# Attention output by three passes of rounded hi and lo operands in place of one fp32 product, in a gated cross-attention and FFN kernel on one core

## The chip, the core and the metric

The kernel runs on one core of a Trainium2 chip. The metric is the device time of one execution in microseconds (us), as the median of several runs. A core has five engines with a queue each, which work strictly in their own order and meet at semaphores: TensorE (PE in the profile, PEld for its weight loads), VectorE (DVE), ScalarE (ACT), GpSimd (POOL) and SyncE (SP), which here issues the large DMAs.

## The reference

For each of 16 batches of 128 rows and 256 columns, with one attention head (the code is cut to what matters):

```python
xn = layernorm(x)
Q = xn @ Wq.T + bq
K = ctx @ Wk.T + bk
scores = where(mask, -inf, Q @ K.T)
attn = softmax(scores)
x1 = x + tanh(g_xattn) * ((attn @ ctx) @ Wo.T + bo)
w = (weights >= 0) * 2.0 - 1.0
y = clip((layernorm(x1) @ w.T) * scale + bias, -100, 100)
out = x1 + tanh(g_ffn) * y
```

All inputs and outputs are fp32.

## The kernel before

The batches go through in 8 groups of two (G = 8, GB = 2). Wq and Wk are folded into one matrix at the start, so that scores = xn times K_sb, where K_sb comes from the context. The context is multiplied with Wo first (Z = ctx x Wo^T, scaled by the gate), and so the attention output is O = P^T x Z, divided by the row sums of P in the residual step on VectorE.

TensorE runs a loop of rounds, written out by hand. In round i it does, in this order: `scores(i)`, the transposes of the context (i+1), of x1 (i-1) and of the normalised x (i+1), `project_Z(i)`, `project_K(i+1)`, `transpose_p(i)`, `ffn(i-1)` and `attend(i)`. The mask's small product at the head of `scores` carries the wait for the group before.

Several products are already made with operands in two parts: ScalarE copies a PSUM result to a tile of type float32r (the rounded hi part), VectorE subtracts that from the PSUM bank and writes the rest (the lo part). `split_cT` and `split_x1T` do so for the context and for x1. `project_Z` and `project_K` then take three products hi x hi, hi x lo and lo x hi, each one pass of TensorE. `attend` is one of the two places in a round that still use full fp32 operands (the other is `scores`): ScalarE copies Z (`evict_Z`) and the transposed P (`evict_PT`) as they are, and two matmuls of fp32 follow, one for each batch. In the trace each such fp32 matmul has two records.

ScalarE's order in round i: cT_hi (i+1), the two exponentials (i), x1T_hi (i-1), xT (i+1), Z (i), PT (i), K (i+1). VectorE's order: `residual(i-1)` (reciprocal, then x1 from ps_O), `max_of_scores(i)`, `scale_ffn_out(i-2)`, `split_cT(i+1)`, `stats_x1(i-1)`, `split_x1T(i-1)`, then the statistics of groups of x that the table `STATS_AT` puts there (groups 2 and 3 in round 0, 4 and 5 in round 1, 6 in round 2, 7 in round 3, none later), and `final(i-2)`, which adds x1 to the clipped FFN output. GpSimd does the small layer norm steps, the normalised x (`xn`), `add_bo`, `bias_and_clip`.

The tile x1_sb has the name x_sb in some rows of the profile, and the lower half of the bank ps_S holds the scores and its upper half the transposed P (`ps_PT`), so that the transposes of P are rows of ps_S.

Of the kernel before, what the change touches and what calls it, by code (L numbers as in the profile page):

```python
# [13 lines left out]
P = 128  # L14
# [7 lines left out]
def gated_xattn_ffn(nc, x, ctx, mask, g_xattn, g_ffn, wq, bq, wk, bk, wo, bo, w_ffn, scale_ffn, bias_ffn, out):  # L22
# [9 lines left out]
    GB = 2  # L32
# [15 lines left out]
    with ExitStack() as stack:  # L48
# [3 lines left out]
        def sem(name):  # L52
            return stack.enter_context(nc.semaphore(name))

        def bank(name):
# [30 lines left out]
        xT = sb("xT", [P, 2, DC, T])  # L86
        cT_hi, cT_lo = sb("cT_hi", [P, 2, DC, T], F32R), sb("cT_lo", [P, 2, DC, T], F32R)
        K_sb = sb("K_sb", [P, 2, DC, T])
        Z_sb = sb("Z_sb", [P, 2, GB, D])
        p_sb, PT_sb = sb("p_sb", [P, 2, GB, P]), sb("PT_sb", [P, 2, GB, P])  # L90
        x1T_hi, x1T_lo = sb("x1T_hi", [P, 2, DC, T], F32R), sb("x1T_lo", [P, 2, DC, T], F32R)


# [43 lines left out]
        bn_x_done, mv_x_done, ve_x_done, rstd_x_done, mr_x_done, off_x_done, xn_done = (  # L137
            sem(n) for n in ("bn_x_done", "mv_x_done", "ve_x_done", "rstd_x_done", "mr_x_done", "off_x_done", "xn_done"))
        bn_1_done, mv_1_done, ve_1_done, rstd_1_done = (sem(n) for n in ("bn_1_done", "mv_1_done", "ve_1_done", "rstd_1_done"))
        cT_hi_done, cT_lo_done, xT_done, K_done, Z_done, PT_done = (  # L140
            sem(n) for n in ("cT_hi_done", "cT_lo_done", "xT_done", "K_done", "Z_done", "PT_done"))
        nmax_done, p_done, recip_done, xb_done, x1_done, x1T_hi_done, x1T_lo_done = (
            sem(n) for n in ("nmax_done", "p_done", "recip_done", "xb_done", "x1_done", "x1T_hi_done", "x1T_lo_done"))
        f_scaled_done, f_biased_done, f_clip_done, out_done = (
# [29 lines left out]
        @block.scalar  # L174
        def _(act):
            act.dma_start(bq_col[:], bq.rearrange("(p c) -> p c", c=DC)).then_inc(bqk_loaded, 16)
            act.dma_start(bk_col[:], bk.rearrange("(p c) -> p c", c=DC)).then_inc(bqk_loaded, 16)
            for k, v in enumerate((g_xattn, g_ffn)):
                act.dma_start(gate_row[:, k:k + 1], row(v)).then_inc(gate_loaded, 16)
            act.dma_start(mask_u8[:], mask).then_inc(mask_loaded, 16)  # L180
            for tile, v in ((bo_row, bo), (sc_row, scale_ffn), (bi_row, bias_ffn)):
                act.dma_start(tile[:], row(v)).then_inc(rows_loaded, 16)

            def evict_cT_hi(g):
                act.wait_ge(cT_prod, g + 1)
                nc.scalar.copy(cT_hi[:, g % 2], ps_cT).then_inc(cT_hi_done, 1)  # L186

            def evict_xT(g):
                act.wait_ge(xT_prod, g + 1)
                nc.scalar.copy(xT[:, g % 2], ps_xT).then_inc(xT_done, 1)  # L190

            def evict_K(g):
                act.wait_ge(kbias_ready, 1)
                act.wait_ge(K_prod, g + 1)
                for c in range(DC):
                    nc.scalar.activation(K_sb[:, g % 2, c], ps_K[:, c], ACT.Identity, bias=kbias[:, c:c + 1]  # L196
                                         ).then_inc(K_done, 1)

            def evict_Z(g):
                act.wait_ge(Z_prod, g + 1)  # L200
                nc.scalar.copy(Z_sb[:, g % 2], ps_Z).then_inc(Z_done, 1)

            def exp(g):
                act.wait_ge(nmax_done, g + 1)
                for b in range(GB):
                    r = g * GB + b
                    nc.scalar.activation(p_sb[:, g % 2, b], ps_S[b], ACT.Exp, bias=nmax[:, r:r + 1],  # L207
                                         accum_out=psum_p[:, r:r + 1]).then_inc(p_done, 1)

            def evict_PT(g):  # L210
                act.wait_ge(PT_prod, g + 1)
                nc.scalar.copy(PT_sb[:, g % 2], ps_PT).then_inc(PT_done, 1)

            def evict_x1T_hi(g):
                act.wait_ge(x1T_prod, g + 1)
                nc.scalar.copy(x1T_hi[:, g % 2], ps_x1T).then_inc(x1T_hi_done, 1)

            evict_cT_hi(0)
            for c in range(DC):
                act.wait_ge(ps_wqk_ready, c + 1)  # L220
                nc.scalar.copy(wqk_hi[:, c], ps_wqk[c]).then_inc(wqk_hi_ready, 1)
            act.wait_ge(ps_kbias_ready, 1)
            nc.scalar.copy(kbias[:], s_bank[:, 0:DC]).then_inc(kbias_ready, 1)
            act.wait_ge(ps_gate_ready, 1)
            nc.scalar.activation(tanh_g[:], o_bank[:, 0:2], ACT.Tanh).then_inc(tanh_ready, 1)
            act.wait_ge(tanh_ready, 1)
            act.wait_ge(ps_woT_ready, 1)
            nc.scalar.activation(woT_hi[:], ps_woT, ACT.Identity, scale=tanh_g[:, 0:1]).then_inc(woT_hi_ready, 1)
            evict_K(0)
            evict_xT(0)  # L230
            act.wait_ge(ps_rows_ready, 1)
            nc.scalar.activation(bo_g[:], x1T_bank[:, 0:D], ACT.Identity, scale=tanh_g[:, 0:1]).then_inc(bo_g_ready, 1)
            for i in range(G + 1):
                if i + 1 < G:
                    evict_cT_hi(i + 1)
                if i < G:
                    exp(i)
                if i >= 1:
                    evict_x1T_hi(i - 1)
                if i + 1 < G:  # L240
                    evict_xT(i + 1)
                if i < G:
                    evict_Z(i)
                    evict_PT(i)
                if i + 1 < G:
                    evict_K(i + 1)
                if i == 0:
                    nc.scalar.activation(sc_g[:], x1T_bank[:, D:2 * D], ACT.Identity, scale=tanh_g[:, 1:2]
                                         ).then_inc(sc_g_ready, 1)
                    act.wait_ge(ps_bi_ready, 1)  # L250
                    nc.scalar.activation(bi_g[:], f_bank[:, 0:D], ACT.Identity, scale=tanh_g[:, 1:2]).then_inc(bi_g_ready, 1)
                    act.wait_ge(ps_wT_ready, 1)
                    nc.scalar.copy(wT[:], ps_x1T).then_inc(wT_ready, 1)
# [86 lines left out]
        def _(dve):  # L340
# [20 lines left out]
            def split_cT(g):  # L361
                dve.wait_ge(cT_hi_done, g + 1)
                nc.vector.tensor_tensor(cT_lo[:, g % 2], ps_cT, cT_hi[:, g % 2].bitcast(F32), ALU.subtract
                                        ).then_inc(cT_lo_done, 1)

            def split_x1T(g):
                dve.wait_ge(x1T_hi_done, g + 1)
                nc.vector.tensor_tensor(x1T_lo[:, g % 2], ps_x1T, x1T_hi[:, g % 2].bitcast(F32), ALU.subtract  # L368
                                        ).then_inc(x1T_lo_done, 1)
# [55 lines left out]
            for i in range(G + 2):  # L425
                if 1 <= i <= G:
                    residual(i - 1)
                if i < G:
                    max_of_scores(i)
                if i >= 2:  # L430
                    scale_ffn_out(i - 2)
                if i == 0:
                    dve.wait_ge(w_loaded, 16)
                    nc.vector.tensor_scalar(w_sign2[:], w_sb[:], 0.0, 2.0, ALU.is_ge, ALU.mult).then_inc(sign2_done, 1)
                    dve.wait_ge(sign2_done, 1)
                    nc.vector.tensor_reduce(w_sum[:], w_sign2[:], AX.X, ALU.add).then_inc(w_sum_done, 1)
                if i + 1 < G:
                    split_cT(i + 1)
                if i == 0:
                    dve.wait_ge(w_sum_done, 1)  # L440
                    nc.vector.tensor_scalar(w_mean[:], w_sum[:], 1.0 / D, None, ALU.mult).then_inc(w_mean_done, 1)
                    dve.wait_ge(w_mean_done, 1)
                    for c in range(DC):
                        nc.vector.tensor_scalar(w_cent[:, c], w_sign2[:, c], w_mean[:, c:c + 1], None, ALU.subtract
                                                ).then_inc(w_cent_ready, 1)
                if 1 <= i <= G:
                    stats_x1(i - 1)
                    split_x1T(i - 1)
                for g in STATS_AT.get(i, ()):
                    stats_x(g)  # L450
                if i >= 2:
                    final(i - 2)

        @block.tensor
        def _(pe):
# [45 lines left out]

            def project_Z(g):
                if g >= 1:
                    pe.wait_ge(Z_done, g)
                else:
                    pe.wait_ge(woT_lo_ready, 1)
                for b in range(GB):
# [6 lines left out]

            def scores(g):
                if g >= 1:
                    pe.wait_ge(PT_done, g)
                else:
                    pe.wait_ge(kbias_ready, 1)
                    pe.wait_ge(mask_ready, 1)  # L520
# [14 lines left out]
                last.then_inc(PT_prod, 1)  # L535

            def attend(g):
                pe.wait_ge(PT_done, g + 1)
                pe.wait_ge(Z_done, g + 1)
                if g >= 1:  # L540
                    pe.wait_ge(x1_done, GB * g)
                else:
                    pe.wait_ge(tanh_ready, 1)
                for b in range(GB):
                    last = nc.tensor.matmul(ps_O[:, b], PT_sb[:, g % 2, b], Z_sb[:, g % 2, b], start=True, stop=True)  # L545
                last.then_inc(O_prod, 1)

            def ffn(g):
# [88 lines left out]
```

## Time and profile before

| | |
|---|---|
| median of 3 runs | 87.29 us (87.25 to 87.45) |
| the profiled execution | 87.51 us |
| its span, first to last instruction | 85.8 us |
| TensorE busy | 71.8 us (84%), 528 matmul records |
| VectorE busy | 52.8 us (62%) |
| ScalarE busy | 36.8 us (43%) |
| GpSimd busy | 58.8 us (69%) |
| one round in the middle of the loop | 7.46 us |

Busy shares are averages over a start of about 14 us, eight rounds and an end of about 11 us. What sets the time is the chain of waits, which names for each stretch the engine whose work ended last. The profiled execution took 87.51 us, 0.22 us more than the median of the runs; 1.71 us of it lie outside the span.

### The profile page before, as it was taken

What the parts mean: (1) busy time and instruction counts of PE and PEld (TensorE: products, weight loads), DVE (VectorE), ACT (ScalarE), POOL (GpSimd) and SP (SyncE); (2) the same over time, 40 slices, a digit from 0 to 9 for tenths busy, and PEclk for the clock granted to TensorE, in tenths of its full rate; (3) what the DMA queues carried; (4) which work ended last, traced back from release to release, by engine and by line L of the source; (5) the groups of instructions that cost most, each with busy time, mean ns of one, the idle gap of its engine ahead of it and who ended that gap; (6) DMA issues with size and microseconds to landing.
All of it is one profiled execution on the core that took longest, in us unless ns stands there. A gap on an engine that the chain in (4) does not pass through costs nothing.

```text
span 85.8 us, 1574 instructions
## 1 busy us (share of the span) xinstructions
PE 71.8 (84%) x528; PEld 65.5 (76%) x528; DVE 52.8 (62%) x153; ACT 36.8 (43%) x98; POOL 58.8 (69%) x105
## 2 busy tenths in 40 slices
PE   2999999597799999999999999999999996635000
PEld 2999997495599979979997997999799795414000
DVE  0057764895059849938974980894498187594430
ACT  0142547655629507552950855395085436020000
POOL 5002888934892905889999688999998819568740
PEclk9999999999999999999999999999999999999555
DMA  0899999920000000030003003000300300300303
GB/s 24 253 344 370 349 348 349 348 72 0 0 0 0 0 0 11 0 113 17 0 0 122 8 0 122 0 0 0 122 8 0 122 0 0 110 12 0 122 0 122
DMA packets 7697, 7.44 MB, mean 87 GB/s; under 512 B 775, under 2 KB 7434, under 8 KB 7690
## 3 DMA queue, kind: packets, MB, share of 16 engines
q1 hardware_dynamic: 7360, 7.34, 26.3%
q8 instruction: 4, 0.07, 0.3%
q10 hardware_dynamic: 330, 0.01, 0.2%
q14 instruction: 3, 0.02, 0.1%
HBM read 5.25 MB, written 2.10 MB: 86 GB/s over the span
## 4 chain that ended last, share of the span: by engine, by line
PE 63%; POOL 14%; DVE 8%; issue 5%; DMA 5%; POOLq 1%; ACTq 0%; DVEq 0%
PE ps_K L465 12%; PE ps_Z L465 11%; PE ps_S L526 9%; PE ps_O L545 8%; PE ps_F L465 8%; DMA bk_col<-in_L_xattn_bk_dram 5%; PE ps_xT L460 4%; PE ps_x1T L460 4%; PE ps_cT L460 3%; POOL xn L284 3%; POOL f_biased L302 3%; POOL mask_sel L318 2%; DVE f_scaled L391 2%; PE ps_S L534 2%; PE ps_S L521 2%
## 5 line engine op out<-in xcount | busy, mean ns | idle before, releaser
L302 POOL TENSOR_TENSOR f_biased<-f_scaled,bi_g 128x256 f32<-128x256 f32 x16 | 11.4, 734 | 8.6 <-DVE f_scaled L391 8.6
L383 DVE SCALAR_TENSOR_TENSOR x_sb<-ps_O,recip_p,xb_sb 128x256 f32<-128x256 f32 x16 | 7.0, 479 | 14.1 <-PE ps_O L545 11.9
L186 ACT CAST cT_hi<-ps_cT 128x512 fp32r<-128x512 f32 x8 | 4.7, 585 | 17.9 <-PE ps_cT L460 17.9
L296 POOL TENSOR_TENSOR xb_sb<-x_sb,bo_g 128x256 f32<-128x256 f32 x16 | 11.3, 727 | 0.0
L465 PE MATMUL ps_F<-wT,x1T_hi 128*128 128x256 f32 x32 | 8.7, 304 | 2.3 <-DVE x1T_lo L368 2.3
L284 POOL TENSOR_SCALAR xn<-x_sb,rstd_x,off_x 128x256 f32<-128x256 f32 x16 | 9.9, 624 | 0.5
L465 PE MATMUL ps_Z<-woT_hi,cT_hi 128*128 128x256 f32 x32 | 9.6, 299 | 0.0
L526 PE MATMUL ps_S<-K_sb,xT 128*128 128x128 f32 x64 | 9.3, 288 | 0.0
L465 PE MATMUL ps_K<-cT_hi,wqk_hi 128*128 128x256 f32 x32 | 9.1, 284 | 0.0
L465 PE MATMUL ps_K<-cT_hi,wqk_lo 128*128 128x256 f32 x32 | 9.0, 282 | 0.0
L465 PE MATMUL ps_K<-cT_lo,wqk_hi 128*128 128x256 f32 x32 | 9.0, 281 | 0.0
L465 PE MATMUL ps_Z<-woT_lo,cT_hi 128*128 128x256 f32 x32 | 8.9, 277 | 0.0
L465 PE MATMUL ps_Z<-woT_hi,cT_lo 128*128 128x256 f32 x32 | 8.9, 277 | 0.0
L526 PEld LDWEIGHTS ps_S<-K_sb,xT 128*128 128x128 f32 x64 | 7.7, 191 | 1.1 <-ACT xT L190 0.2
L545 PE MATMUL ps_O<-Z_sb,PT_sb 128*128 128x256 f32 x32 | 8.2, 378 | 0.0
L465 PEld LDWEIGHTS ps_F<-wT,x1T_hi 128*128 128x128 f32 x32 | 6.0, 188 | 2.8 <-DVE x1T_lo L368 2.8
L465 PE MATMUL ps_F<-wT,x1T_lo 128*128 128x256 f32 x32 | 8.0, 282 | 0.0
L396 DVE TENSOR_TENSOR out_sb<-f_clip,x_sb 128x512 f32<-128x512 f32 x8 | 5.5, 691 | 3.8 <-POOL f_clip L306 3.8
L391 DVE SCALAR_TENSOR_TENSOR f_scaled<-ps_F,rstd,sc_g 128x256 f32<-128x256 f32 x16 | 6.9, 475 | 0.9 <-POOL rstd L291 0.9
L269 POOL TENSOR_SCALAR ve_x<-mv_x 128x4 f32<-128x4 f32 (+1 forms) x5 | 1.5, 292 | 8.8 <-DVE mv_x L349 8.6
L196 ACT ACTIVATE K_sb<-ps_K,kbias 128x256 f32<-128x256 f32 x16 | 6.7, 477 | 0.7 <-PE ps_K L465 0.7
L207 ACT ACTIVATE p_sb<-ps_S,nmax 128x128 f32<-128x128 f32 x16 | 5.8, 369 | 2.5 <-DVE nmax L373 2.5
(94 smaller groups left out, 193.5 us busy)
## 6 DMA issues: line engine op xcount, KB each, us to landing
ctx_sb<-in_ctx_dram SPq DMA_DIRECT2D x8, 256.0 KB, 6.5
x_sb<-in_x_dram SPq DMA_DIRECT2D x8, 256.0 KB, 6.3
out_dram<-out_sb SPq DMA_DIRECT2D x8, 256.0 KB, 2.1
wq_sb<-in_L_xattn_Wq_dram SPq DMA_DIRECT2D x1, 256.0 KB, 3.0
wk_sb<-in_L_xattn_Wk_dram SPq DMA_DIRECT2D x1, 256.0 KB, 3.8
wo_sb<-in_L_xattn_Wo_dram SPq DMA_DIRECT2D x1, 256.0 KB, 4.8
w_sb<-in_L_ffn_weights_dram SPq DMA_DIRECT2D x1, 256.0 KB, 5.6
bq_col<-in_L_xattn_bq_dram ACTq DMA_DIRECT2D x1, 1.0 KB, 3.2
```

Source lines behind the costliest of these rows:

```text
L196: nc.scalar.activation(K_sb[:, g % 2, c], ps_K[:, c], ACT.Identity, bias=kbias[:, c:c + 1]).then_inc(K_done, 1)
L207: nc.scalar.activation(p_sb[:, g % 2, b], ps_S[b], ACT.Exp, bias=nmax[:, r:r + 1], accum_out=psum_p[:, r:r + 1]).then_inc(p_done, 1)
L284: nc.gpsimd.tensor_scalar(xn[:, g % 3, b], x_sb[:, r], rstd_x[:, r:r + 1], off_x[:, r:r + 1], ALU.mult, ALU.add).then_inc(xn_done, 1)
L296: nc.gpsimd.tensor_tensor(xb_sb[:, r], x_sb[:, r], bo_g[:], ALU.add).then_inc(xb_done, 1)
L302: nc.gpsimd.tensor_tensor(f_biased[:, r], f_scaled[:, r], bi_g[:], ALU.add).then_inc(f_biased_done, 1)
L383: nc.vector.scalar_tensor_tensor(out=x1_sb[:, r], in0=ps_O[:, b], scalar=recip_p[:, r:r + 1], in1=xb_sb[:, r], op0=ALU.mult, op1=ALU.add). ...
L391: nc.vector.scalar_tensor_tensor(out=f_scaled[:, r], in0=ps_F[:, b], scalar=rstd_1[:, r:r + 1], in1=sc_g[:], op0=ALU.mult, op1=ALU.mult).t ...
L396: nc.vector.tensor_tensor(out_sb[:, rows(g)], f_clip[:, g % 2], x1_sb[:, rows(g)], ALU.add).then_inc(out_done, 1)
L460: last = nc.tensor.transpose(dst[:, c, b * P:(b + 1) * P], src[:, b, c * P:(c + 1) * P], ident[:])
L465: last = nc.tensor.matmul(dst, lhsT, rhs, start=(n == 0), stop=(n == len(pairs) - 1))
L526: last = nc.tensor.matmul(ps_S[b], xT[:, g % 2, c, b * P:(b + 1) * P], K_sb[:, g % 2, c, b * P:(b + 1) * P], start=False, stop=(b == GB - ...
L545: last = nc.tensor.matmul(ps_O[:, b], PT_sb[:, g % 2, b], Z_sb[:, g % 2, b], start=True, stop=True)
```

## The change

Z and the transposed P are now kept in two rounded parts each. ScalarE's two copies write float32r tiles Z_hi and PT_hi. VectorE gets two new instructions in every round, `split_Z(i)` behind `split_x1T(i-1)` and ahead of the statistics, and `split_PT(i)` behind the statistics and ahead of `final(i-2)`. `attend` makes three products for each batch in place of one, and waits for the lo parts.

```diff
-        Z_sb = sb("Z_sb", [P, 2, GB, D])
-        p_sb, PT_sb = sb("p_sb", [P, 2, GB, P]), sb("PT_sb", [P, 2, GB, P])
+        Z_hi, Z_lo = sb("Z_hi", [P, 2, GB, D], F32R), sb("Z_lo", [P, 2, GB, D], F32R)
+        p_sb = sb("p_sb", [P, 2, GB, P])
+        PT_hi, PT_lo = sb("PT_hi", [P, 2, GB, P], F32R), sb("PT_lo", [P, 2, GB, P], F32R)
...
-                nc.scalar.copy(Z_sb[:, g % 2], ps_Z).then_inc(Z_done, 1)
+                nc.scalar.copy(Z_hi[:, g % 2], ps_Z).then_inc(Z_hi_done, 1)
...
-                nc.scalar.copy(PT_sb[:, g % 2], ps_PT).then_inc(PT_done, 1)
+                nc.scalar.copy(PT_hi[:, g % 2], ps_PT).then_inc(PT_hi_done, 1)
...
+            def split_Z(g):
+                dve.wait_ge(Z_hi_done, g + 1)
+                nc.vector.tensor_tensor(Z_lo[:, g % 2], ps_Z, Z_hi[:, g % 2].bitcast(F32), ALU.subtract
+                                        ).then_inc(Z_lo_done, 1)
+
+            def split_PT(g):
+                dve.wait_ge(PT_hi_done, g + 1)
+                nc.vector.tensor_tensor(PT_lo[:, g % 2], ps_PT, PT_hi[:, g % 2].bitcast(F32), ALU.subtract
+                                        ).then_inc(PT_lo_done, 1)
...
                 if 1 <= i <= G:
                     stats_x1(i - 1)
                     split_x1T(i - 1)
+                if i < G:
+                    split_Z(i)
                 for g in STATS_AT.get(i, ()):
                     stats_x(g)
+                if i < G:
+                    split_PT(i)
                 if i >= 2:
                     final(i - 2)
...
-                    pe.wait_ge(Z_done, g)
+                    pe.wait_ge(Z_lo_done, g)
...
-                    pe.wait_ge(PT_done, g)
+                    pe.wait_ge(PT_lo_done, g)
...
-                pe.wait_ge(PT_done, g + 1)
-                pe.wait_ge(Z_done, g + 1)
+                pe.wait_ge(PT_lo_done, g + 1)
+                pe.wait_ge(Z_lo_done, g + 1)
...
-                    last = nc.tensor.matmul(ps_O[:, b], PT_sb[:, g % 2, b], Z_sb[:, g % 2, b], start=True, stop=True)
+                    p_hi, p_lo, z_hi, z_lo = (t[:, g % 2, b] for t in (PT_hi, PT_lo, Z_hi, Z_lo))
+                    last = accumulate(ps_O[:, b], [(p_hi, z_hi), (p_hi, z_lo), (p_lo, z_hi)])
```

On VectorE, the rows of round 1 from the lo part of x1 on stood like this before (`bn_x` and `mv_x` are the statistics of groups 4 and 5, the last row is the x1 of group 1):

```order
L368 TENSOR_TENSOR x1T_lo<-ps_x1T,x1T_hi 128x512
L345 BN_STATS bn_x<-x_sb 128x6 x2
L349 BN_AGGR mv_x<-bn_x 128x2 x2
L345 BN_STATS bn_x<-x_sb 128x6 x2
L349 BN_AGGR mv_x<-bn_x 128x2 x2
L377 RECIPROCAL recip_p<-psum_p 128x2
L383 SCALAR_TENSOR_TENSOR x_sb<-ps_O,recip_p,xb_sb 128x256 x2
```

And so they stand in the changed kernel:

```order
L380 TENSOR_TENSOR x1T_lo<-ps_x1T,x1T_hi 128x512
L370 TENSOR_TENSOR Z_lo<-ps_Z,Z_hi 128x512
L347 BN_STATS bn_x<-x_sb 128x6 x2
L351 BN_AGGR mv_x<-bn_x 128x2 x2
L347 BN_STATS bn_x<-x_sb 128x6 x2
L351 BN_AGGR mv_x<-bn_x 128x2 x2
L375 TENSOR_TENSOR PT_lo<-ps_S,PT_hi 128x256
L389 RECIPROCAL recip_p<-psum_p 128x2
L395 SCALAR_TENSOR_TENSOR x_sb<-ps_O,recip_p,xb_sb 128x256 x2
```

The subtraction for P, on which `attend` of the same round waits, stands behind both groups of statistics.

On TensorE, the end of round 1 in the changed kernel, from the last product of the FFN on, reads so (before, one row `L545 MATMUL ps_O<-Z_sb,PT_sb 128x256 x2` stood in place of the six products into ps_O):

```order
L481 MATMUL ps_F<-wT,x1T_lo 128x256
L481 MATMUL ps_O<-Z_hi,PT_hi 128x256
L481 MATMUL ps_O<-Z_lo,PT_hi 128x256
L481 MATMUL ps_O<-Z_hi,PT_lo 128x256
L481 MATMUL ps_O<-Z_hi,PT_hi 128x256
L481 MATMUL ps_O<-Z_lo,PT_hi 128x256
L481 MATMUL ps_O<-Z_hi,PT_lo 128x256
```

Nothing else moves on TensorE; ScalarE and GpSimd keep their order.

## Rows read from the trace of the kernel before

**Rows 1.** The page, part 4: the chain that ended last, by engine.

```profile
PE 63%; POOL 14%; DVE 8%; issue 5%; DMA 5%; POOLq 1%; ACTq 0%; DVEq 0%
```

**Rows 2.** The chain in order of time, round 6: start us, us, what.

```profile
63.33 1.38 PE ps_Z L465 x12
...
67.32 0.87 PE ps_O L545 x4
```

**Rows 3.** Timeline of TensorE: attend of rounds 0, 1, 2, 6, 7; once what follows.

```profile
22.40 1.03 PE L545 MATMUL ps_O<-Z_sb,PT_sb 128*128 128x256 f32 x4
...
29.86 1.03 PE L545 MATMUL ps_O<-Z_sb,PT_sb 128*128 128x256 f32 x4
...
37.32 1.03 PE L545 MATMUL ps_O<-Z_sb,PT_sb 128*128 128x256 f32 x4
...
67.16 1.03 PE L545 MATMUL ps_O<-Z_sb,PT_sb 128*128 128x256 f32 x4
68.12 0.28 PE L521 MATMUL ps_S<-mask_sel,ones_b 16*128 16x258 bf16 x1
...
73.30 1.03 PE L545 MATMUL ps_O<-Z_sb,PT_sb 128*128 128x256 f32 x4
```

**Rows 4.** Timeline of VectorE and TensorE, round 7: a product that waited for a lo part.

```profile
71.52 0.66 DVE L368 TENSOR_TENSOR x1T_lo<-ps_x1T,x1T_hi 128x512 fp32r<-128x512 f32 x1
...
72.24 0.39 PE L465 MATMUL ps_F<-wT,x1T_hi 128*128 128x256 f32 x1 [0.72 <-DVE x1T_lo L368]
72.46 0.28 PE L465 MATMUL ps_F<-wT,x1T_lo 128*128 128x256 f32 x1
```

**Rows 5.** Timeline of ScalarE and VectorE, round 1: a split that waited for its hi part.

```profile
25.20 0.58 ACT L186 CAST cT_hi<-ps_cT 128x512 fp32r<-128x512 f32 x1 [2.02 <-PE ps_cT L460]
...
25.81 0.69 DVE L363 TENSOR_TENSOR cT_lo<-ps_cT,cT_hi 128x512 fp32r<-128x512 f32 x1 [0.62 <-ACT cT_hi L186]
26.42 0.74 DVE L355 BATCH_NORM_STATS2 bn<-x_sb 128x6 f32<-128x256 f32 x2
```

**Rows 6.** Groups of instructions (busy us, mean ns of one): a split of 256 columns.

```profile
L413 DVE TENSOR_TENSOR wqk_lo<-ps_K,wqk_hi 128x256 fp32r<-128x256 f32 x1 | 0.4, 425 | 0.0
```

**Rows 7.** Timeline of ScalarE: copies of Z (L201) and PT (L212), rounds 0, 1, 2 and 6.

```profile
18.70 0.58 ACT L201 COPY Z_sb<-ps_Z 128x512 f32<-128x512 f32 x1 [0.80 <-PE ps_Z L465]
...
27.45 0.59 ACT L201 COPY Z_sb<-ps_Z 128x512 f32<-128x512 f32 x1
...
34.91 0.58 ACT L201 COPY Z_sb<-ps_Z 128x512 f32<-128x512 f32 x1
36.56 0.37 ACT L212 COPY PT_sb<-ps_S 128x256 f32<-128x256 f32 x1 [1.07 <-PE ps_S L534]
...
66.40 0.37 ACT L212 COPY PT_sb<-ps_S 128x256 f32<-128x256 f32 x1 [1.07 <-PE ps_S L534]
```

**Rows 8.** Timeline of VectorE behind split_x1T, in rounds 1 and 2.

```profile
27.87 0.74 DVE L345 BATCH_NORM_STATS2 bn_x<-x_sb 128x6 f32<-128x256 f32 x2
...
29.60 0.13 DVE L377 RECIPROCAL recip_p<-psum_p 128x2 f32<-128x2 f32 x1
...
35.40 0.74 DVE L345 BATCH_NORM_STATS2 bn_x<-x_sb 128x6 f32<-128x256 f32 x2
```

**Rows 9.** Timeline of GpSimd and VectorE: rounds 2 and 3, then round 5.

```profile
37.57 1.09 POOL L284 TENSOR_SCALAR xn<-x_sb,rstd_x,off_x 128x256 f32<-128x256 f32 x2
...
39.03 0.69 POOL L291 TENSOR_TENSOR rstd<-ve,half 128x2 f32<-128x2 f32 x1
...
40.02 0.86 DVE L391 SCALAR_TENSOR_TENSOR f_scaled<-ps_F,rstd,sc_g 128x256 f32<-128x256 f32 x2
...
58.70 1.62 POOL L284 TENSOR_SCALAR xn<-x_sb,rstd_x,off_x 128x256 f32<-128x256 f32 x2
58.74 0.69 DVE L396 TENSOR_TENSOR out_sb<-f_clip,x_sb 128x512 f32<-128x512 f32 x1 [0.73 <-POOL f_clip L306]
```

More of the change, by code:

```diff
@@ L139, in gated_xattn_ffn @@
         bn_1_done, mv_1_done, ve_1_done, rstd_1_done = (sem(n) for n in ("bn_1_done", "mv_1_done", "ve_1_done", "rstd_1_done"))
-        cT_hi_done, cT_lo_done, xT_done, K_done, Z_done, PT_done = (
-            sem(n) for n in ("cT_hi_done", "cT_lo_done", "xT_done", "K_done", "Z_done", "PT_done"))
+        cT_hi_done, cT_lo_done, xT_done, K_done, Z_hi_done, Z_lo_done, PT_hi_done, PT_lo_done = (
+            sem(n) for n in ("cT_hi_done", "cT_lo_done", "xT_done", "K_done", "Z_hi_done", "Z_lo_done", "PT_hi_done",
+                             "PT_lo_done"))
         nmax_done, p_done, recip_done, xb_done, x1_done, x1T_hi_done, x1T_lo_done = (
```

## The prediction

> **What bounds the kernel now.** I read the page's chain first: 63% of it is TensorE, GpSimd and VectorE have 14% and 8% [rows 1]. In the order of time those two stand at the start and the end, and from round 1 to round 6 the chain is TensorE alone, piece by piece, with `attend` as one piece of 0.87 us for its two fp32 products [rows 2]. The timeline of TensorE says the same: `attend` begins at 29.86 in round 1 and at 37.32 in round 2, 7.46 us apart, and by round 6 at 67.16, five times 7.46 after round 1 [rows 3]. So whatever TensorE is spared in a round comes off the time, and whatever it is made to wait is added, as long as nothing else is as late. Then I looked for what `attend` will wait for: the two copies on ScalarE [rows 7] and VectorE's place in its own order [rows 8].
>
> **What is removed.** Two fp32 products cost 0.87 us [rows 2]. In their place come six products of 256 columns of float32r. The same shape and type, with the same pattern of operands, is `project_Z`: 12 in 1.38 us, 0.115 us each [rows 2], so six cost 0.69 us, and 0.18 us a round are spared. The other end is 0.12 us for one: from 72.46 to 73.30 lie seven slots [rows 3, 4], which would spare 0.15. I take 0.18 for the same operand pattern; in eight rounds that is 1.44 us. ScalarE's two copies stay as long as they were: a rounding copy of 512 columns took 0.58 us, the plain one 0.58 to 0.59 [rows 5, 7].
>
> **What is added.** Two subtractions a round on VectorE, and with them a longer way to `attend`. Its prices:
> - From the end of a copy on ScalarE to a waiting split: copy 25.20 + 0.58 = 25.78, split at 25.81, so 0.03 us [rows 5].
> - `split_Z`, 512 columns: the next instruction starts 0.61 us after the split (25.81 to 26.42) [rows 5].
> - `split_PT`, 256 columns: 0.42 us to its end, by the same subtraction out of a PSUM bank at that width [rows 6]. It can't be above the 0.69 of twice the width [rows 5].
> - From the end of a split to a waiting TensorE: 71.52 + 0.66 = 72.18, and the records start at 72.24, 0.06 later. The second product starts 0.22 after the first where a slot is 0.12, so 0.10 us of the first weight load lie open [rows 4]. Together 0.16.
> - The statistics of two groups: 27.87 to 29.60, 1.73 us [rows 8], so 0.87 for one group.
>
> Round 1, the dear one. Z_hi is there at 27.45 + 0.59 + 0.03 = 28.07 [rows 7], while VectorE is free at 27.87 [rows 8]. `split_Z` from 28.07 to 28.68, two groups of statistics to 30.41, `split_PT` to 30.83, first product of `attend` in effect at 30.99. It stood at 29.86 [rows 3]: 1.13 us of stall, less 0.18, **+0.95**.
>
> Rounds 2 and 3, one group each. Z_hi at 34.91 + 0.58 + 0.03 = 35.52, against 35.40 where VectorE is free; `split_Z` to 36.13, statistics to 37.00. PT_hi would allow 36.56 + 0.37 + 0.03 = 36.96 [rows 7], so the statistics are 0.04 late; `split_PT` to 37.42, product at 37.58, before 37.32. Stall 0.26, less 0.18: +0.08, twice, **+0.16**.
>
> Rounds 4 to 6, no statistics. `split_Z` is over before P is transposed. PT_hi at 66.40 + 0.37 + 0.03 = 66.80 [rows 7], `split_PT` to 67.22, product at 67.38, before 67.16 [rows 3]. Stall 0.22, less 0.18: +0.04, three times, **+0.12**. The FFN products between the transposes of P and `attend` hide the copy today with some room, but not the copy and a subtraction.
>
> Round 0 has two groups of statistics too, but TensorE waits there anyway for the constants of the FFN. `split_Z` from 18.70 + 0.58 + 0.03 = 19.31, with both statistics to 21.65, `split_PT` to 22.07, released at 22.13; `attend` starts at 22.40 [rows 3, 7]. No stall, **-0.18**. If that cover were gone, nothing before 22.40 would change, since 0.27 us are left.
>
> Round 7: the split of x1 ends at 72.18, `split_Z` and `split_PT` behind it take some 0.61 + 0.42, less the overlap of 0.06 with the end of the one before, to 73.15, product at 73.31 against 73.30 today, because the FFN products have waited for VectorE themselves [rows 3, 4]. No stall, **-0.18**.
>
> Sum: 0.95 + 0.16 + 0.12 - 0.18 - 0.18 = +0.87 us. On the profiled execution of 87.51 that is 88.38; it stood 0.22 above the median of the runs, so **88.2 us** against 87.29.
>
> **What is moved.** `final(i-2)` and the reciprocal now stand behind `split_PT`, ahead of the x1 of the round, which waits for ps_O. In round 2 they end at 37.42 + 0.69 + 0.13 = 38.24 [rows 8, 9], and `attend` is not over before 37.58 + 0.69 = 38.27. Hidden, with next to nothing left in full lengths; real starts overlap a little, which helps. If it is not hidden, it costs what it overhangs, 0.1 us a round. The waits of `project_Z` and `scores` for the lo parts of the round before are met long before.
>
> A second effect of the move: `final` reads two tiles of SBUF. In round 5 it lay over `xn` on GpSimd, and the pair took 1.62 us where the same pair takes 1.09 in round 2 [rows 9]. Now it starts about 37.36 in round 2, over the `xn` at 37.57, so rstd of group 1 ends at 39.03 + 0.69 + 0.53 = 40.25, when VectorE wants it at 40.02 + 0.08 = 40.10 [rows 9]. 0.15 late; round 3's `split_Z` has 0.12 of room (35.52 less 35.40, one round on), so 0.03 are left. I count it at nothing, 0.15 at most. The Trainium skill (SBUF — State Buffer, "SBUF: two separate sides") has a rule for it: a VectorE instruction with two SBUF inputs and a GpSimd one that reads SBUF lock each other out of a shared port for a whole instruction. By that rule the added splits, with one input in PSUM, hold nobody. The 0.53 us of round 5 agree with the rule, less than a whole `final` because the two started nearly together.
>
> **Rivals.**
> (a) Faster: the weight loads of the rounded products are pulled forward. Today the mask's product follows `attend` after 0.96 us (67.16 to 68.12), 0.09 more than the 0.87 of the piece [rows 2, 3]. If float32r products let the mask's load go early, 0.09 come off seven times, 0.63; if the first load of `attend` isn't open after a wait, 0.10 off six times, 0.60. Together -1.23, which gives +0.87 - 1.23 = -0.36, 86.9 us. It decides the sign from 0.87 on. Against it stands the waiting product whose load was open [rows 4]. The Trainium skill (TensorE: Matmul & The Clock Gate, the table of specs at its head) says that TensorE's queue pulls weight loads ahead of running matmuls within a window. Applied to the mask's load alone, that would make the sum +0.24. Chance of the whole 0.08, of one half (87.5 to 87.6) 0.10.
> (b) Slower by more: VectorE becomes the chain. If a subtraction out of the bank of P took up to 0.69, the six stalls grow by 0.27 each, and the shifted `final` and reciprocal overhang by as much: +1.6, 89.8 us. For it: VectorE has hardly 0.03 us left at 38.24. Against: the price at this width is in the trace [rows 6]. A tenth of a microsecond more a round, 88.8, is likelier than the whole. Chance of more than 88.9: 0.09.
> (c) No net change: VectorE takes the statistics of round 1 early enough. That would need 0.95 us of the stall to vanish; it leaves -0.08, 87.2 us. For it speaks only that the statistics are not needed so soon; their place in the order is fixed, in front of `split_PT`. Chance 0.05.
> The forecast itself, 87.8 to 88.9, has 0.68.
>
> **How the numbers follow.** The bounds of the unknown prices: 0.15 for 0.18 adds 0.24; the late rstd adds up to 0.15; an overhang of 0.1 in six rounds adds 0.6, hence 88.9 above with some of them together. Below, the half of (a) that concerns the first load gives 87.56, the other half 87.53; the range ends at 87.4 and leaves out the whole of (a) and (c). It holds 0.68 + 0.10 and a little. A measurement of this kernel tells about 0.2% from no change, 0.17 us: faster is below 87.12, slower above 87.46. Faster: the whole of (a) and part of (c), 0.11. Same: the rest of (c) and the lower edge of the halves, 0.07. Slower: 0.82.
>
> **What the changed kernel's profile would show.** TensorE in round 1: a gap of about 1.1 us between the last FFN product and the first product into ps_O, released by PT_lo; its releaser right ahead of it on VectorE the statistics. Gaps of about 0.2 in rounds 2 to 6, none in rounds 0 and 7. Rounds of 7.5 us where they were 7.46, round 1 about 8.4. Six products into ps_O in 0.69 us. `split_PT` rows of 0.42, `split_Z` of 0.66 to 0.69. I am wrong if round 1 has no such gap, if the mask's product follows the last product of `attend` sooner than it did, or if the x1 of a round starts later after `attend` than now, which would show `final` in the way.

## The result, and the profile after

| | before | changed |
|---|---|---|
| profiled execution | 87.51 us | 88.65 us |
| median of the runs | 87.27 us (4) | 88.96 us (4, 88.29 to 91.11) |
| changed over before | | 1.0147, 95% interval 1.0095 to 1.0199 |
| both again, beside experiments 5, 6 and 9 | 87.33 us (18) | 88.52 us (6), 1.0143, interval 1.0116 to 1.0170 |

The kernel became 1.4% slower. Executions over 1.5% longer than the fastest of their kernel, most of them with a lower granted clock of TensorE, stand in the medians but in no ratio; without its 91.11 the changed kernel has a median of 88.65 us. The profiled executions stand 1.14 us apart, the spans 1.1 us (86.9 and 85.8), and the ratios make it 1.25 to 1.28 us. The prediction had +0.87 us and 88.2.

The chain that ended last, part 4 of the page of the changed kernel:

```profile
PE 57%; POOL 14%; DVE 11%; issue 5%; DMA 4%; ACT 3%; POOLq 1%; ACTq 0%; DVEq 0%
```

TensorE held 63% before [rows 1]. VectorE has gained three points, and ScalarE comes in. Where that happened is to be seen in the rounds. The stretches below run from one mask product to the next, rounds 1 to 6 (columns: us of the stretch, then busy us and instructions of PE, PEld, DVE, ACT and POOL, granted clock, share and rate of the DMAs):

```profile
23.13:31.55 8.42, 7.58 (x62) 7.12 (x61) 6.25 (x20) 3.96 (x11) 6.25 (x12) 1.00 0.00 1
31.55:39.14 7.59, 7.59 (x62) 7.15 (x62) 6.68 (x19) 3.96 (x11) 4.64 (x8) 1.00 0.02 3
39.14:46.73 7.59, 7.59 (x63) 7.15 (x62) 6.69 (x19) 3.95 (x11) 7.15 (x13) 1.00 0.10 36
46.73:54.27 7.54, 7.54 (x63) 7.11 (x62) 5.92 (x15) 3.95 (x11) 6.28 (x11) 1.00 0.11 37
54.27:61.84 7.57, 7.57 (x63) 7.14 (x62) 5.93 (x15) 3.97 (x11) 7.13 (x13) 1.00 0.10 35
61.84:69.39 7.55, 7.55 (x62) 7.12 (x62) 6.21 (x15) 3.96 (x11) 6.10 (x10) 1.00 0.11 37
sum 46.26, PE 45.42 PEld 42.78 DVE 37.68 ACT 23.74 POOL 37.56; mean PE 7.57 PEld 7.13 DVE 6.28 ACT 3.96 POOL 6.26
```

A round took 7.46 us before, six of them 44.76; now they take 46.26, +1.50. Of this +0.96 are in round 1, +0.13 each in rounds 2 and 3, +0.08 to +0.11 in the others. Note that "PE busy" fills rounds 2 to 6 completely although there is a stall in each of them: the ends of products are modelled in the profile and cover a gap of this size. Only the distance of starts shows it.

TensorE's timeline at the end of round 1, and of round 6 (68.23 is the last product of the FFN):

```profile
29.52 0.28 PE L481 MATMUL ps_F<-wT,x1T_lo 128*128 128x256 f32 x1
30.64 0.39 PE L481 MATMUL ps_O<-Z_hi,PT_hi 128*128 128x256 f32 x1 [0.84 <-DVE PT_lo L375]
30.87 0.28 PE L481 MATMUL ps_O<-Z_lo,PT_hi 128*128 128x256 f32 x1
...
31.34 0.28 PE L481 MATMUL ps_O<-Z_hi,PT_lo 128*128 128x256 f32 x1
31.55 0.28 PE L537 MATMUL ps_S<-mask_sel,ones_b 16*128 16x258 bf16 x1
...
68.23 0.28 PE L481 MATMUL ps_F<-wT,x1T_lo 128*128 128x256 f32 x1
68.48 0.38 PE L481 MATMUL ps_O<-Z_hi,PT_hi 128*128 128x256 f32 x1
68.70 0.28 PE L481 MATMUL ps_O<-Z_lo,PT_hi 128*128 128x256 f32 x1
...
69.39 0.28 PE L537 MATMUL ps_S<-mask_sel,ones_b 16*128 16x258 bf16 x1
```

Here a slot is the distance of two starts in the stream. In round 1 the first product of `attend` starts 1.12 us after the last one of the FFN, where a slot is 0.12; its weight load lies open for another 0.11 (30.64 to 30.87 in place of 0.12). In round 6 it is 0.25 and 0.10. From the second product to the sixth it goes by 0.12 (30.87 to 31.34), and the mask's product follows the last one after 0.21, so 0.09 us of its load lie open as before [rows 2, 3]. The rows of the weight loads (PEld) in round 1 show it directly:

```profile
31.23 0.19 PEld L481 LDWEIGHTS ps_O<-Z_hi,PT_lo 128*128 128x128 f32 x1
31.55 0.09 PEld L537 LDWEIGHTS ps_S<-mask_sel,ones_b 16*128 16x128 bf16 x1
```

The load of the last product of `attend` starts 0.11 us ahead of its product (31.34), the mask's load together with its product (31.55).

VectorE's timeline in round 1, and in round 6, from `split_Z` on:

```profile
27.86 0.69 DVE L370 TENSOR_TENSOR Z_lo<-ps_Z,Z_hi 128x512 fp32r<-128x512 f32 x1
28.46 0.74 DVE L347 BATCH_NORM_STATS2 bn_x<-x_sb 128x6 f32<-128x256 f32 x2
...
30.20 0.39 DVE L375 TENSOR_TENSOR PT_lo<-ps_S,PT_hi 128x256 fp32r<-128x256 f32 x1
30.50 0.16 DVE L389 RECIPROCAL recip_p<-psum_p 128x2 f32<-128x2 f32 x1
...
68.00 0.42 DVE L375 TENSOR_TENSOR PT_lo<-ps_S,PT_hi 128x256 fp32r<-128x256 f32 x1 [0.75 <-ACT PT_hi L214]
68.34 1.12 DVE L408 TENSOR_TENSOR out_sb<-f_clip,x_sb 128x512 f32<-128x512 f32 x1
69.39 0.15 DVE L389 RECIPROCAL recip_p<-psum_p 128x2 f32<-128x2 f32 x1
69.60 0.88 DVE L395 SCALAR_TENSOR_TENSOR x_sb<-ps_O,recip_p,xb_sb 128x256 f32<-128x256 f32 x2
```

In round 1 nothing is idle between `split_Z` and `split_PT`: 1.74 us of statistics. In round 6 VectorE waits 0.75 us for ScalarE's copy. Also `final` took 1.12 us there, and x1 followed the reciprocal at once, without the idle time that it had in the other rounds.

### The profile page after: what moved, and what is told of

The parts are those of the page before. It is cut to its first block, busy times and chain, and to the rows that moved or that the text cites. A ratio compares the mean times of both kernels' runs of the same rounds, so it can differ in the third digit from the quotient of the medians.

```text
span 86.9 us, 1622 instructions
## 1 busy us (share of the span) xinstructions
PE 72.9 (84%) x544; PEld 67.4 (78%) x544; DVE 60.8 (70%) x169; ACT 36.8 (42%) x98; POOL 58.4 (67%) x105
## 4 chain that ended last, share of the span: by engine, by line
PE 57%; POOL 14%; DVE 11%; issue 5%; DMA 4%; ACT 3%; POOLq 1%; ACTq 0%; DVEq 0%
PE ps_K L481 10%; PE ps_Z L481 10%; PE ps_S L542 9%; PE ps_O L481 8%; PE ps_F L481 7%; DMA bk_col<-in_L_xattn_bk_dram 4%; PE ps_xT L476 3%; PE ps_x1T L476 3%; PE ps_cT L476 3%; POOL xn L286 3%; POOL f_biased L304 3%; POOL mask_sel L320 2%; DVE bn_x L347 2%; DVE f_scaled L403 2%; PE ps_S L537 2%
## 5 line engine op out<-in xcount | busy, mean ns | idle before, releaser
L481 PE MATMUL ps_F<-wT,x1T_hi 128*128 128x256 f32 x32 | 9.2, 316 | 2.3 <-DVE x1T_lo L380 2.3
L481 PE MATMUL ps_F<-wT,x1T_lo 128*128 128x256 f32 x32 | 8.5, 296 | 0.0
L271 POOL TENSOR_SCALAR ve_x<-mv_x 128x4 f32<-128x4 f32 (+1 forms) x5 | 1.0, 192 | 10.0 <-DVE mv_x L351 9.8
L293 POOL TENSOR_TENSOR rstd<-ve,half 128x2 f32<-128x2 f32 x8 | 6.8, 846 | 0.7
```

Of the source, the lines that this page charges most:

```text
L293: nc.gpsimd.tensor_tensor(rstd_1[:, rows(g)], ve_1[:, rows(g)], half[:, rows(g)], ALU.pow).then_inc(rstd_1_done, 1)
L481: last = nc.tensor.matmul(dst, lhsT, rhs, start=(n == 0), stop=(n == len(pairs) - 1))
```

## The experiments

Each was run beside the kernel before; a ratio is to that kernel. All diffs are against the changed kernel unless it says otherwise.

**1. The products alone.** The splits are out, and attend waits for the hi parts, as do `project_Z` and `scores` where they waited for the lo parts. All three products are hi x hi; the lo parts are left out of the computation.

```diff
-                if i < G:
-                    split_Z(i)
...
-                if i < G:
-                    split_PT(i)
...
-                pe.wait_ge(PT_lo_done, g + 1)
-                pe.wait_ge(Z_lo_done, g + 1)
+                pe.wait_ge(PT_hi_done, g + 1)
+                pe.wait_ge(Z_hi_done, g + 1)
...
-                    last = accumulate(ps_O[:, b], [(p_hi, z_hi), (p_hi, z_lo), (p_lo, z_hi)])
+                    last = accumulate(ps_O[:, b], [(p_hi, z_hi), (p_hi, z_hi), (p_hi, z_hi)])
```

> Part of the change done alone: attend takes three float32r products for each batch, but all three are hi x hi, the two subtractions on VectorE are left out, and attend waits for the hi parts as the kernel before waits for its copies. The lo parts are left out of the computation, so the output is not the reference's. Theory (the change spares product time on TensorE and loses more by waiting): no stall in any round, and eight times what six products cost less than 0.87 us. By 0.115 us for one that is 0.18 a round and 1.44 in all, 85.8 us; by the 0.12 that the changed kernel's trace shows it is 0.15 a round and 1.2 in all, about 86.1. Rival (the products themselves are the loss, for instance by open weight loads): no gain, 87.3 or more.

Measured: 86.23 us, ratio 0.9878 (0.9832 to 0.9924), -1.1 us. TensorE's timeline at the end of round 6:

```profile
66.21 0.88 PE L477 MATMUL ps_O<-Z_hi,PT_hi 128*128 128x256 f32 x6
67.02 0.28 PE L533 MATMUL ps_S<-mask_sel,ones_b 16*128 16x258 bf16 x1
```

From the start of attend to the mask's product it is 0.81 us, against 0.96 before [rows 3]: 0.15 spared, six slots of 0.12 and the same 0.09 open. The products do bring what they should, by the upper of my two prices. A whole round is only 0.11 us shorter (7.35 for 7.46), because the unchanged products of `project_Z` took 1.50 us here and 1.46 before, from their first start to what follows.

**2. The splits alone.** Z and P stay fp32, two fp32 products, but both subtractions are made and waited for (the subtractions lose their bitcasts, which the diff leaves out).

```diff
-        Z_hi, Z_lo = sb("Z_hi", [P, 2, GB, D], F32R), sb("Z_lo", [P, 2, GB, D], F32R)
+        Z_hi, Z_lo = sb("Z_hi", [P, 2, GB, D]), sb("Z_lo", [P, 2, GB, D], F32R)
...
-        PT_hi, PT_lo = sb("PT_hi", [P, 2, GB, P], F32R), sb("PT_lo", [P, 2, GB, P], F32R)
+        PT_hi, PT_lo = sb("PT_hi", [P, 2, GB, P]), sb("PT_lo", [P, 2, GB, P], F32R)
...
-                    last = accumulate(ps_O[:, b], [(p_hi, z_hi), (p_hi, z_lo), (p_lo, z_hi)])
+                    last = accumulate(ps_O[:, b], [(p_hi, z_hi)])
```

> The other part alone: Z and the transposed P stay fp32 and attend makes its two fp32 products, but VectorE does both subtractions in their places and attend waits for them (the subtractions run on fp32 tiles and give zeros that nobody reads). Theory: the stalls alone, 1.13 in round 1, 0.26 in rounds 2 and 3, 0.22 in rounds 4 to 6, 2.3 us in all, 89.6. Together with the products alone that must give the whole change: the two sums add up to 1.1 us. Rival (VectorE has become the chain, with the final addition and the reciprocal in the way of x1): the sum does not add up, since here attend is longer and leaves VectorE more room; then 89.0 or less.

Measured: 89.67 us, ratio 1.0269 (1.0215 to 1.0322), +2.35 us. With experiment 1 that makes -1.09 + 2.35 = +1.26 by the medians, where the change has 1.43% of 87.3, 1.25. The parts add up within what the medians tell (each ratio is uncertain by 0.5%), and its rounds 1 to 6 are 2.34 us longer than before where 2.31 of stalls were forecast. VectorE is not the chain on its own account.

**3. The subtraction for P between the two groups of statistics.**

```diff
                 if i < G:
                     split_Z(i)
-                for g in STATS_AT.get(i, ()):
+                stats = STATS_AT.get(i, ())
+                for g in stats[:1]:
                     stats_x(g)
                 if i < G:
                     split_PT(i)
+                for g in stats[1:]:
+                    stats_x(g)
```

> The changed kernel with one move: the subtraction for P stands behind the first group of statistics of the round and ahead of the second, which only matters in rounds 0 and 1. Theory (0.95 us are lost in round 1 because two groups of statistics stand in front of the subtraction): the stall of round 1 falls from 1.13 to some 0.27, so 0.86 us less than the changed kernel, 87.8 on its profiled 88.65. Rival (round 1 is late for its order on VectorE as a whole, and the statistics only move behind): x1 of round 1 starts later after attend, and most of the 0.86 stays.

The first four executions gave no ratio (the profiled one took 87.54 us), so the kernel was run again:

> The kernel with the subtraction for P between the two groups of statistics again, since its first runs gave no ratio. Its trace had 7.61 us in round 1 where the changed kernel had 8.42, so 0.8 less than the changed kernel: 87.7, 0.3 to 0.5% above the kernel before.

Measured: 87.65 us (12 runs), ratio 1.0023 (0.9992 to 1.0054). VectorE's and TensorE's timelines, round 1 (29.22 is the last product of the FFN):

```profile
29.05 0.39 DVE L375 TENSOR_TENSOR PT_lo<-ps_S,PT_hi 128x256 fp32r<-128x256 f32 x1
29.35 0.74 DVE L347 BATCH_NORM_STATS2 bn_x<-x_sb 128x6 f32<-128x256 f32 x2
...
30.62 0.88 DVE L395 SCALAR_TENSOR_TENSOR x_sb<-ps_O,recip_p,xb_sb 128x256 f32<-128x256 f32 x2 [0.26 <-PE ps_O L484]
...
29.22 0.28 PE L484 MATMUL ps_F<-wT,x1T_lo 128*128 128x256 f32 x1
29.49 0.39 PE L484 MATMUL ps_O<-Z_hi,PT_hi 128*128 128x256 f32 x1
```

The stretch of round 1:

```profile
22.77:30.40 7.63, 7.63 (x62) 7.10 (x62) 6.25 (x20) 3.96 (x11) 6.53 (x13) 1.00 0.00 1
```

The gap of round 1 is down from 1.12 to 0.27, and x1 still waits 0.26 us for `attend`, so the second group of statistics is hidden behind the subtraction. Round 1 went from 8.42 to 7.63 us, by 0.79 where 0.86 were expected at first. By the ratios the kernel is 1.0 us faster than the changed one (1.0023 beside 1.0143), give or take 0.4. So one instruction's place was the greater part of the loss, 0.79 of the 1.14 us between the profiled executions, and what is left is no difference that this measurement shows.

**4. P transposed earlier.** On TensorE alone:

```diff
-                if i + 1 < G:
-                    project_K(i + 1)
                 if i < G:
                     transpose_p(i)
+                if i + 1 < G:
+                    project_K(i + 1)
```

> The changed kernel with one move on TensorE: the transposes of P stand ahead of project_K, so that project_K's 1.43 us lie between them and attend as well. Theory: rounds 4 to 6 lose their stall of 0.22 each, since the copy and the subtraction are then long done; rounds 1 to 3 keep theirs, because there the statistics on VectorE are what the subtraction stands behind. 0.66 us less than the changed kernel, 88.0 on its profiled 88.65. Rival (the short stalls are all one delay, from the copy to the product): rounds 1 to 3 gain too, 87.5 or less.

Measured: 87.71 us, ratio 1.0036 (1.0009 to 1.0063). The rounds, 1 to 4:

```profile
22.71:31.16 8.45, 7.63 (x62) 7.17 (x62) 6.24 (x20) 3.96 (x11) 6.40 (x13) 1.00 0.00 1
31.16:38.72 7.56, 7.56 (x63) 7.11 (x62) 6.68 (x19) 3.96 (x11) 4.62 (x8) 1.00 0.01 3
38.72:46.31 7.59, 7.59 (x63) 7.16 (x62) 6.69 (x19) 3.96 (x11) 7.15 (x13) 1.00 0.11 36
46.31:53.67 7.36, 7.36 (x62) 7.11 (x61) 5.83 (x15) 3.96 (x11) 6.10 (x11) 1.00 0.12 40
```

Round 4 (and 5 and 6 like it, 7.37 each) is 0.2 shorter, and rounds 1 to 3 are what they were. The six rounds are 0.56 us shorter together, for 0.66 expected; the ratios say 0.93 with an uncertainty of about 0.3, and in the profiled executions 0.3 of the difference lie before round 0 began. So there are two kinds of stall: in rounds 4 to 6 the way from the transposes over the copy and the subtraction, in 1 to 3 the statistics ahead of the subtraction.

**5. The same move on the kernel before.** Same diff, applied to the kernel before.

> The kernel before with only the transposes of P moved ahead of project_K. Theory: attend never waited there, and the move by itself does nothing: 87.3, within 0.2%. Rival (the order itself is better for TensorE, and what the variants with this move gain is not the end of a stall): 0.5 us or more faster.

Measured: 87.06 us, ratio 0.9979 (0.9953 to 1.0004). No difference that this measurement shows; its interval reaches to -0.4 us, and its rounds 1 to 6 lasted 7.45 or 7.46 as before. So the order by itself is not what experiment 4 gained.

**6. Both moves.** P transposed earlier, and:

```diff
                 if i < G:
                     split_Z(i)
+                    split_PT(i)
                 for g in STATS_AT.get(i, ()):
                     stats_x(g)
-                if i < G:
-                    split_PT(i)
```

> The changed kernel with both moves: on TensorE the transposes of P stand ahead of project_K, and on VectorE the subtraction for P stands right behind the one for Z, ahead of all statistics. Theory: the copy and the subtraction are over before the FFN's products are, in every round, so no round stalls, and eight times 0.15 us are spared against the kernel before: 86.1 to 86.3 us. VectorE must still finish the statistics, the final addition and the reciprocal before x1 is due; by its rows it does in round 1 by about 0.1 us. Rival (VectorE with two more instructions a round is too full for its order): x1 comes late in rounds 1 to 3 and the time is 86.8 or more.

Measured: 86.61 us, ratio 0.9923 (0.9893 to 0.9954). The change becomes a gain. It stays 0.3 above the forecast, for two reasons. Rounds 2 to 6 lasted 7.36 to 7.37 where 7.31 were forecast; the Z products, 1.46 us in the kernel before from their first start to the start of what follows, took 1.50. And round 1 lasted 7.62, since the transposes of the normalised x waited for GpSimd (timelines of GpSimd and TensorE, then the stretches of rounds 1 and 2):

```profile
21.52 0.19 POOL L271 TENSOR_SCALAR ve_x<-mv_x 128x4 f32<-128x4 f32 x1 [4.03 <-DVE mv_x L351]
...
23.49 1.09 POOL L286 TENSOR_SCALAR xn<-x_sb,rstd_x,off_x 128x256 f32<-128x256 f32 x2
...
24.64 0.66 PE L475 MATMUL ps_xT<-ident,xn 128*128 128x128 f32 x4
...
22.34:29.96 7.62, 7.56 (x63) 7.07 (x62) 6.06 (x19) 3.96 (x11) 6.73 (x13) 1.00 0.00 1
29.96:37.32 7.36, 7.36 (x62) 7.11 (x61) 6.87 (x22) 3.96 (x11) 4.42 (x8) 1.00 0.01 3
```

xn ends at 24.58, the transposes start at 24.64, 2.30 us into the round where it is 2.07 in round 2. GpSimd had waited for the statistics of round 0, which stand behind both subtractions there.

**7. Both moves, and the statistics first in round 0.** The diff is against the kernel of experiment 6.

```diff
+                stats = STATS_AT.get(i, ())
+                if i == 0:
+                    for g in stats:
+                        stats_x(g)
                 if i < G:
                     split_Z(i)
                     split_PT(i)
-                for g in STATS_AT.get(i, ()):
-                    stats_x(g)
+                if i > 0:
+                    for g in stats:
+                        stats_x(g)
```

> The variant with both moves (P transposed ahead of project_K, the subtraction for P ahead of the statistics), and in round 0 alone the statistics first, as TensorE waits there anyway. In the variant's trace round 1 lasted 7.62 us where rounds 2 to 6 lasted 7.36, because the transposes of the normalised x waited 0.22 us for GpSimd, which got the statistics of round 0 late. Theory: this wait goes, 0.2 to 0.25 less than the variant, 86.1 to 86.4 beside its 86.2 to 86.8. Rival (the wait only moves to VectorE's subtraction for P in round 0): the same as the variant.

Measured: 86.25 us (6 runs, 85.93 to 86.39), ratio 0.9873 (0.9835 to 0.9910), the fastest version of the full computation here and level with the products alone. The first two of its rounds:

```profile
22.67:30.04 7.37, 7.37 (x63) 7.12 (x62) 6.06 (x19) 3.96 (x11) 5.32 (x10) 1.00 0.00 1
30.04:37.40 7.36, 7.36 (x62) 7.11 (x61) 6.87 (x22) 3.96 (x11) 4.42 (x8) 1.00 0.01 3
```

Round 1 is 0.25 us shorter than in experiment 6, as expected, and the wait for xn is gone. The ratios stand 0.44 us apart, but their intervals overlap, so only the trace shows the size. All six rounds last 7.36 or 7.37 us now, 0.09 to 0.10 less than before and not 0.15, with the Z products at 1.50 or 1.51 us.

**8. The subtraction first, P transposed in its old place.** The diff of experiment 6, without the move on TensorE.

> The changed kernel with the subtraction for P ahead of all statistics, P transposed in its old place. Theory: attend of rounds 1 to 6 stalls 0.22 each, and in round 1 the 1.73 us of statistics now end about 0.65 after x1 is due, of which the transposes ahead of those of x1 hide 0.45: about 0.6 to 0.7 more than the kernel before, 87.9 to 88.0. Rival (only what stands ahead of the subtraction counts, what stands behind is free): 0.4 more than the kernel before, 87.7.

Measured: 88.64 us, ratio 1.0144 (1.0090 to 1.0197): 0.6 to 0.7 more than expected, and no better than the changed kernel. Its trace shows both late ends. VectorE in round 1, TensorE in rounds 0 and 1, and the stretches of rounds 1 and 2:

```profile
33.03 0.42 DVE L375 TENSOR_TENSOR PT_lo<-ps_S,PT_hi 128x256 fp32r<-128x256 f32 x1 [0.74 <-ACT PT_hi L214]
33.37 0.74 DVE L347 BATCH_NORM_STATS2 bn_x<-x_sb 128x6 f32<-128x256 f32 x2
...
35.27 0.88 DVE L395 SCALAR_TENSOR_TENSOR x_sb<-ps_O,recip_p,xb_sb 128x256 f32<-128x256 f32 x2
...
22.70 0.38 PE L549 MATMUL ps_S<-ident,p_sb 128*128 128x128 f32 x2
...
28.90 0.66 PE L475 MATMUL ps_xT<-ident,xn 128*128 128x128 f32 x4 [0.68 <-POOL xn L286]
...
25.97:34.41 8.44, 7.76 (x62) 7.09 (x62) 5.52 (x16) 4.07 (x11) 7.29 (x13) 1.00 0.00 1
34.41:42.17 7.76, 7.76 (x63) 7.11 (x62) 6.95 (x23) 3.97 (x11) 4.59 (x9) 1.00 0.01 3
```

x1 of round 1 starts without any idle time before it, 0.86 us after the mask's product (34.41) where it is 0.20 to 0.23 in the changed kernel, and round 2 lasts 7.76 us, 0.2 more than the changed kernel's, as expected. What I had missed is the wait for xn: in round 0 the statistics now stand behind a subtraction that itself waits for the late transposes of P, and GpSimd hands xn over 0.85 us late (2.93 us into round 1, where it is 2.08 in the changed kernel). In this execution the granted clock was 0.5 (1.2 GHz) from 15.51 to 22.34 us. The transposes of P in round 0 and all behind them came later, at full clock, and from them to `attend` it took 2.39 us for 2.38 in the changed kernel's trace, so the lateness of xn does not come from the clock. The expectation's 0.6 to 0.7 and these 0.85 give 1.5; the trace's rounds 1 to 6 are 1.66 us longer than before, which less 0.15 each for rounds 0 and 7 is 1.36; the measured ratio is 1.26 us, with both inside its interval. With P transposed early this wait is 0.22, with experiment 7 it is gone.

**9. The final addition ahead of the subtraction.**

```diff
-                if i < G:
-                    split_PT(i)
                 if i >= 2:
                     final(i - 2)
+                if i < G:
+                    split_PT(i)
```

> The changed kernel with the final addition back ahead of the subtraction for P. Theory (from the copy of P, or from the end of the statistics where these are later, everything in front of the subtraction adds to attend's start): in rounds 2 and 3 the statistics already set the start, so the 0.60 us of the addition are added twice; in rounds 4 to 6 the addition fits in front of the copy of P, but for 0.05 in round 5, where it waits for the clipped values. 1.2 to 1.3 more than the changed kernel, 89.9. Rival (the addition behind the subtraction is itself what costs, by holding up the reciprocal and x1): 88.6 or less.

Measured: 90.40 us, ratio 1.0373 (1.0335 to 1.0411), about 2.0 us more than the changed kernel by the ratios. TensorE's timeline, `attend` of rounds 2 and 7:

```profile
38.41 0.39 PE L481 MATMUL ps_O<-Z_hi,PT_hi 128*128 128x256 f32 x1 [0.59 <-DVE PT_lo L375]
...
75.89 0.39 PE L481 MATMUL ps_O<-Z_hi,PT_hi 128*128 128x256 f32 x1 [0.39 <-DVE PT_lo L375]
```

In round 2 the gap from the last FFN product (37.53) is 0.88 where it was 0.26: the 0.6 of the addition, entire. Round 3 has the same, rounds 4 to 6 have nothing, and the six rounds together 1.20 us, as expected. The expectation left out round 7, where VectorE sets the pace: the addition is in front there as well and adds about 0.6 (a gap of 0.67 for 0.12, and 0.10 of open load). That is the difference between 89.9 and 90.4.

## Why the prediction was right, point by point

The cause and its place were right, in direction and nearly in size. Rounds 1 to 6 were forecast at +1.23 us and measured at +1.50.
- The dear round: +0.95 predicted, +0.96 measured. It met so closely because two small errors cancel: the stall was 1.11 us for 1.13, and the products spared 0.15 for 0.18. Experiment 3 shows that the second group of statistics alone is 0.79 of it.
- Rounds 2 to 6: the stalls were 0.24 in rounds 2 to 5 and 0.23 in round 6 (0.13 to 0.14 in front and 0.10 of open load), for the predicted 0.26 and 0.22. Experiment 4 separates the two kinds as the steps had them. All six stalls come to 2.30 us for the forecast 2.31.
- The mis-sized term is the product. I took 0.115 us by the pattern of `project_Z`, and it was 0.12, the other end that the prediction kept: 0.15 spared for 0.18, over eight rounds 0.24 us. The working's stalls with it give 0.87 + 0.24 = 1.11 against the 1.14 of the profiled executions and the 1.25 to 1.28 of the ratios.
- What stood nowhere in the sum: the unchanged Z products took 1.46 to 1.50 us from their first start to that of the K products, by round, 0.14 us more in rounds 1 to 6 of the changed kernel. In the profiled execution it is nearly cancelled by the start, where round 0 began 0.05 later and lost 0.14 less waiting for xn than the kernel before. That wait was anything from 0.35 to 1.10 us over the traces, so that 1.11 and 1.14 meet so closely is luck.
- Rounds 0 and 7 had no stall, and were shorter by their product. The cover held, but what filled round 0 was closer than the text said: it looked only at `attend` there, and not at the statistics behind `split_Z`, on which GpSimd and then xn of round 1 wait. In the changed kernel xn was there 0.39 us before TensorE wanted it (24.82 and 25.21); in experiments 6 and 8 it was late.
- `final` behind the subtraction is hidden, and its place is worth 2 us (experiment 9). By full lengths the prediction left it 0.03 us; x1 in fact waited another 0.50 us for `attend` in rounds 2 to 5, since instructions overlap and `attend` ends after its last slot. In round 6 `final` took 1.12 us, and x1 followed with nothing between, but still 0.21 us after the mask's product where it was 0.20 in round 5, so it cost nothing. The predicted late rstd in round 3 did not come: `final` lay over xn in round 2 and that pair took 1.43 us where 1.09 is usual, but f_scaled started 0.34 after the maximum, as in the other rounds. In experiments 6, 7 and 8 it did come (f_scaled 0.51 to 0.53 after the maximum), and round 3 was no longer for it: 7.37 us in experiments 6 and 7, like its neighbours.
- Rival (a), earlier weight loads, fell on both halves: 0.10 open after a wait in each of rounds 1 to 6, 0.09 open in front of the mask. So the rule of the Trainium skill (TensorE: Matmul & The Clock Gate, table of specs) on loads pulled ahead of running products did not show at the step to the mask's product, fp32 or float32r. Why this load is not ahead, when those of `attend` in the stream are by 0.11 us, no run shows. Rival (b) fell with experiment 2 and by the rows of the subtraction itself, 0.39 to 0.43 us. Rival (c) was wrong for this order. Its case, the stall of round 1 gone, is nearest to experiment 3, level with the kernel before as (c) had it. That the other short stalls can go as well, for -1.1 us (experiment 7), it did not see.

What stays open: why the Z products go by 1.46 or 1.50 us. It is not the tiles' addresses, since rounds 2 and 4 use the same buffers and had 1.49 and 1.46, nor the splits, since the products alone had 1.50 in rounds 1 to 6. With fp32 operands in `attend` it was 1.45 or 1.46 in rounds 1 to 6 of both traces without the splits.

## What to carry to other kernels

Splitting an operand moves work from TensorE onto the way between two of its products, so the new instruction's place in the other engine's order decides more than its length: here 0.42 us of subtraction cost 1 us behind statistics that were wanted only later, and nothing ahead of them once P was transposed earlier as well (experiments 6 and 7; without that, experiment 8 was no better). Before such a change, lengthen the stretch of independent products between the transpose and its use by what the copy and the subtraction take. When an instruction is moved in front of others, follow each of those to who waits for it, on every engine and in the first and last rounds too, where the order is the same but the pace is another's.

## What the runs showed of the hardware

A VectorE addition of two SBUF tiles and a GpSimd instruction that reads SBUF hold each other up in both directions. GpSimd's `xn` pair took 1.43 us under `final` in round 2, and in round 6 it was VectorE that was held (timelines of VectorE in round 2 and of GpSimd in rounds 2 and 6, changed kernel; 1.43 is what this second pair always takes):

```profile
38.09 0.68 DVE L408 TENSOR_TENSOR out_sb<-f_clip,x_sb 128x512 f32<-128x512 f32 x1
...
38.31 1.43 POOL L286 TENSOR_SCALAR xn<-x_sb,rstd_x,off_x 128x256 f32<-128x256 f32 x2
...
67.49 1.43 POOL L298 TENSOR_TENSOR xb_sb<-x_sb,bo_g 128x256 f32<-128x256 f32 x2
```

`final` started at 68.34 and ended at 69.46, 0.54 after the second addition of the pair was over at 68.92, where alone it takes 0.68. In round 2 `final` ended at 38.77 and the first xn at 39.20, 0.43 later, where alone it takes 0.55. The Trainium skill (SBUF — State Buffer, "SBUF: two separate sides") says that whichever starts first keeps the shared port for its whole instruction; the rows agree, but for the 0.12 to 0.14 us by which the held instruction is done sooner than a full length after the other. Recorded starts do not settle who was first when they lie close: in round 5 of the kernel before, xn started 0.04 us ahead of `final` and was still the one held [rows 9]. The splits, with one input in PSUM, were not lengthened by GpSimd: 0.39 to 0.43 and 0.68 to 0.69 us in all rounds, also in round 6, where `split_PT` (68.00 to 68.43) lay wholly under the pair of 67.49.

A product whose operand has just been waited for costs 0.10 us more than one in the stream: 0.22 to 0.23 us to the next start for 0.12, in rounds 1 to 6 of the changed kernel, and 0.32 for 0.22 with the fp32 products of experiment 2. In a chain of one wait a round that is as much as two thirds of what the rounded products spare. A wait is not the only place with an open load: the first product of `project_Z`, behind the transposes and without a stall, has 0.20 us to the next where 0.11 to 0.12 is usual (25.57 to 25.77 in round 1 of the changed kernel).
